# Router logits in four column groups, and the up product behind gate, in a fused decoder layer

## The reference

```python
x = layernorm(x + attn(x))                    # one head; theta from sigmoid, tanh, relu; softmax
x = layernorm(x + cross_attn(x, ctx))         # 16 heads of 16, within chunks of 64 tokens
x = layernorm(x + moe(x))

# moe, for each token:
logits = tokens @ router_weight.T             # 32 experts
scores = sigmoid(logits)
sfc    = scores + router_bias
# the best 2 of 4 groups of 8 experts, by the sum of their two best; in them the best 4 experts
topk_w = scores[topk] / scores[topk].sum() * 2.5
mixed  = sum_k topk_w[k] * down_k(silu(gate_k(t)) * up_k(t))
shared = (silu(t @ shared_gate_w.T) * (t @ shared_up_w.T)) @ shared_down_w.T
out    = mixed + shared
```

## Time and profile before

| | |
|---|---|
| time, median of 3 runs | 827.7 us (824.57 to 830.9) |
| profiled execution: span on the page | 830.3 us |
| PE busy | 765.2 us, 92% |
| VectorE busy | 581.5 us, 70% |
| ScalarE busy | 494.4 us, 60% |
| GpSimd busy | 368.0 us, 44% |
| mean granted TensorE clock | 0.969 |

### The profile page before, as it was taken

The page is one execution under the profiler, slowest core; times in us unless marked ns, Lnnn a source line. Parts: engine busy times, 40 slices in busy tenths (PEclk is TensorE's granted clock), DMA queues, the critical chain, the costliest instruction groups (busy, mean ns, idle before and its releaser), DMA issues.

```text
span 830.3 us, 21803 instructions
## 1 busy us (share of the span) xinstructions
PE 765.2 (92%) x8308; PEld 665.4 (80%) x8308; DVE 581.5 (70%) x2094; ACT 494.4 (60%) x1166; POOL 368.0 (44%) x437
## 2 busy tenths in 40 slices
PE   7969899999999999999997756799999999999986
PEld 6758788888888888888876636799999999998554
DVE  2345487898889888898888763366666666665486
ACT  0546666767767767777654414467676766764143
POOL 0101214334543355334554662366666666665142
PEclk9999999999999999999989877799999999999999
DMA  6582221332433334332113436755555555552996
GB/s 233 156 214 84 84 84 53 108 118 92 142 121 110 120 99 129 120 110 89 66 65 103 142 111 189 270 172 167 177 172 173 171 169 170 176 168 83 370 401 241
DMA packets 69642, 124.95 MB, mean 150 GB/s; under 512 B 9665, under 2 KB 43329, under 8 KB 69282
## 3 DMA queue, kind: packets, MB, share of 16 engines
q1 hardware_dynamic: 51394, 81.60, 32.1%
q0 software_dynamic: 13776, 37.77, 12.6%
q10 hardware_dynamic: 4368, 4.20, 1.4%
HBM read 73.16 MB, written 50.36 MB: 149 GB/s over the span
## 4 chain that ended last, share of the span: by engine, by line
PE 78%; DMA 7%; DVE 6%; SPq 5%; issue 2%; POOL 1%; ACT 1%; ACTq 0%; DVEq 0%
PE banks L538 17%; PE banks L284 10%; PE banks L545 8%; PE banks L386 3%; PE banks L377 3%; PE banks L354 3%; PE banks L322 3%; PE banks L367 3%; PE banks L489 3%; SPq L567 3%; PE banks L331 3%; PE banks L463 3%; PE banks L498 3%; PE banks L339 3%; DMA w_expert_tile<-y 2%; PE banks L429 2%
## 5 line engine op out<-in xcount | busy, mean ns | idle before, releaser
L1293 POOL DMA_INDIRECT y<-yb_tile,idcol_tile x159 | 152.4, 959 | 112.9 <-DVE yb_tile L1144 110.2
L538 PE MATMUL banks<-xbT_tile,wgu_tile 128*128 128x128 f32 x1272 | 172.0, 280 | 0.0
L538 PEld LDWEIGHTS banks<-xbT_tile,wgu_tile 128*128 128x128 f32 x1272 | 158.6, 196 | 0.1
L1144 DVE SCALAR_TENSOR_TENSOR yb_tile<-banks,rowsb_tile 128x256 f32<-128x256 f32 x159 | 76.9, 484 | 84.2 <-PE banks L545 76.1
L857 ACT ACTIVATE wgu_tile<-w_expert_tile 128x512 f32 x159 | 98.9, 622 | 11.8 <-DVE tab_i_tile L1121 11.8
L545 PE MATMUL banks<-w_expert_tile,hb_tile 128*128 x318 | 96.3, 385 | 5.2 <-DVE hb_tile L1132 5.2
L1271 POOL DMA_INDIRECT routed<-row_tile,idx_tile x64 | 62.5, 976 | 68.8 <-PE banks L399 53.2
L853 ACT ACTIVATE gb_tile<-banks 128x128 f32<-128x128 f32 x159 | 44.1, 277 | 79.1 <-PE banks L538 79.1
L1265 POOL DMA_INDIRECT routed<-row_tile,idx_tile x64 | 61.7, 964 | 31.1 <-issue 18.5
L1246 POOL TENSOR_TENSOR rs_tile<-ve_tile,half_neg_tile 128x2 f32<-128x2 f32 x16 | 11.1, 693 | 143.6 <-DVE ve_tile L960 143.6
L284 PE MATMUL banks<-const_tile,rowsb_tile 128*128 128x128 f32 x318 | 62.2, 278 | 7.1 <-DMA rowsb_tile<-routed 7.1
(11 more groups left out here) (206 smaller groups left out, 1784.4 us busy)
## 6 DMA issues: line engine op xcount, KB each, us to landing
rowsb_tile<-routed SPq DMA_DIRECT2D x159, 129.0 KB, 2.2
w_expert_tile<-y SPq DMA_DIRECT2D x15, 1024.0 KB, 15.0
w_expert_tile<-w_expert SPq DMA_DIRECT2D x16, 768.0 KB, 4.6
cT_tile<-ctxT SPq DMA_DIRECT2D x16, 384.0 KB, 3.2
routed<-zrow_tile SPq DMA_DIRECT2D x1, 4128.0 KB, 22.5
xT_tile<-xT SPq DMA_DIRECT2D x16, 256.0 KB, 3.0
x_sb_tile<-x SPq DMA_DIRECT2D x16, 256.0 KB, 2.7
inner<-hs_tile SPq DMA_DIRECT2D x16, 256.0 KB, 2.3
```

The source lines that it names most:

```text
L538: m = e.matmul(bank[2 + u % 4][:, h * P:(h + 1) * P], wgu[u % WG][:, k * D + h * EI:k * D + (h + 1) * EI], xbT[u % 2][:, k * P:(k + 1) * P ...
L1144: e.scalar_tensor_tensor(yb[n % YS][:, :], bank[6 + u % 2][:, 0:D], rowsb[n % ROWS][:, D:D + 1], rowsb[n % ROWS][:, 0:D], ALU.mult, ALU.ad ...
L1293: e.indirect_dma_start(y, bass.IndirectOffsetOnAxis(ap=idcol[n % ROWS][:, :], axis=0), yb[n % YS][:, :], None).then_inc(SEM[f"st_y{n % YS} ...
```

## The change

Four things, in the routing of one sequence:

1. `pe_router`: before, four products with 128 token columns of x2 as the loaded weights and the 32 router columns as the moving operand; the output has tokens on partitions, 64 columns. Now eight products with the 32 router columns as loaded weights and 64 tokens moving, into four groups of 32 partitions; the output has experts on partitions.
2. `act_sc` takes the tanh of that output into `lg`, which shares its memory with `g8` of the routing, so it now waits for the routing of the sequence before (`v_route`). Then PE brings it back to token rows by two products with pieces of the identity (`pe_scT`), placed behind the scores of the first attention, and DVE makes the sigmoid out of PSUM in a stage of its own (`vec_sc`), placed behind `vec_shb`. Before, that instruction stood at the head of `vec_route`.
3. `pe_up` waits for `v_sc` in place of `a_sc`.
4. `pe_up` moves from in front of `pe_pTa` to behind `pe_gate`.

```diff
         def pe_router(e, i):
             e.wait_ge(SEM["a_x2T"], i + 1)
             e.wait_ge(SEM["ld_w"], 16 * 3)
-            for t in range(T):
-                for k in range(DK):
-                    m = e.matmul(bank[7][:, t * E:(t + 1) * E], x2T[i % 2][:, k, t * P:(t + 1) * P], w_router[:, k, :],
+            for k in range(DK):
+                for j in range(4):
+                    m = e.matmul(bank[7][32 * j:32 * j + 32, 0:CH], w_router[:, k, :], x2T[i % 2][:, k, j * CH:(j + 1) * CH],
                                  start=k == 0, stop=k == DK - 1)
             m.then_inc(SEM["p_router"], 1)
+
+        def pe_scT(e, i):
+            e.wait_ge(SEM["a_sc"], i + 1)
+            own = ident.rearrange("p (t a x) -> p a t x", t=T, a=2)
+            for a in range(2):
+                m = e.matmul(bank[7][a * CH:(a + 1) * CH, CH:CH + T * E], lg[:, :], own[:, a, :, :], start=True, stop=True)
+            m.then_inc(SEM["p_scT"], 1)
...
         def pe_up(e, i):
-            after(e, SEM["a_sc"], min(i + 2, nseq))
+            after(e, SEM["v_sc"], min(i + 2, nseq))
             after(e, SEM["v_hs"], i)
...
-                if live(t - 5):
-                    pe_up(e, t - 5)
+                if live(t - 4):
+                    pe_scT(e, t - 4)
                 if live(t - 2):
                     pe_pTa(e, t - 2)
                 if live(t - 4):
                     pe_gate(e, t - 4)
+                if live(t - 5):
+                    pe_up(e, t - 5)
...
         def act_sc(e, i):
             e.wait_ge(SEM["p_router"], i + 1)
-            e.activation(sc[:, :, :].rearrange("p a b -> p (a b)"), bank[7][:, 0:T * E], ACT.Tanh, scale=0.5)\
+            after(e, SEM["v_route"], i)
+            e.activation(lg[:, :], bank[7][:, 0:CH], ACT.Tanh, scale=0.5)\
                 .then_inc(SEM["a_sc"], 1)
...
+        def vec_sc(e, i, ch):
+            e.wait_ge(SEM["p_scT"], i + 1)
+            e.tensor_scalar(sc[:, :, :].rearrange("p t x -> p (t x)"), bank[7][:, CH:CH + T * E], 0.5, 0.5,
+                            ALU.mult, ALU.add).then_inc(SEM["v_sc"], 1)
+
         def vec_route(e, i, ch):
 
-            e.wait_ge(SEM["a_sc"], i + 1)
-            ch(e.tensor_scalar(sc[:, :, :], sc[:, :, :], 0.5, 0.5, ALU.mult, ALU.add))
+            e.wait_ge(SEM["v_sc"], i + 1)
...
                 if live(t - 2):
                     vec_shb(e, t - 2, ch)
+                if live(t - 4):
+                    vec_sc(e, t - 4, ch)
                 if live(t):
                     vec_th(e, t, ch)
```

More of the change, by code:

```diff
@@ L35 @@
     "p_av1", "p_av2", "p_den", "p_down", "p_gu", "p_k", "p_out2", "p_pTa", "p_pTb", "p_prT", "p_q", "p_rank",
-    "p_router", "p_s1", "p_s2", "p_setup", "p_sg", "p_spread", "p_su", "p_sum", "p_tab", "p_vo", "p_x1T", "p_x2T",
+    "p_router", "p_s1", "p_scT", "p_s2", "p_setup", "p_sg", "p_spread", "p_su", "p_sum", "p_tab", "p_vo", "p_x1T", "p_x2T",
     "p_xbT", "p_z", "st_hs", "st_zrow", "v_adr", "v_fve", "v_h1", "v_hb", "v_hb1", "v_hs", "v_key", "v_msel",
-    "v_mx", "v_mxa", "v_mxb", "v_nblk", "v_nmr", "v_o", "v_onehot", "v_own", "v_r", "v_rden", "v_rep", "v_route",
+    "v_mx", "v_mxa", "v_mxb", "v_nblk", "v_nmr", "v_o", "v_onehot", "v_own", "v_r", "v_rden", "v_rep", "v_route", "v_sc",
     "v_setup", "v_sha", "v_shb", "v_sum", "v_tab", "v_ve1", "v_ve2", "v_yb", "v_zrow",
@@ L202, in build @@
         g8 = sa("g8", [P, T, GRP, 8])
+        lg = g8[:, :, :, :].rearrange("p t g x -> p (t g x)")
         gs = sa("gs", [P, T, GRP + 6])
```

## The result

The changed kernel took 839.7 us (median of four runs, 835.9 to 840.8), the kernel before 828.1 beside it (824.6 to 830.9). The ratio is **1.013, with an interval of 1.009 to 1.017**: slower by about 1.3%.

The account below looks back on a forecast made before the run. PE was taken to bound the kernel, with up filling its wait for DVE's shb. Terms -0.25 + 1.5 + 4.7 + 2.6 + 2.5 - 1.7 = +9.3 us, against 827.7, gave 837.0 us; range 829 to 842.

Parts of the forecast that it names:

- iteration 4: First step, no up yet: DVE had waited 0.53 us for PE's vo, which the shorter router brings forward; -0.25 us.
- iteration 5: Step where the transposes have only 0.37 us behind shb: the wait saves 0.22, up adds 1.73; +1.5 us.
- iteration 16: Late step where PE already waited 0.92 us for shb: up adds 1.73 to 3.46 us, 2.6 taken.
- iteration 17: Late step where PE already waited 1.88 us for shb: up adds 1.4 us at full clock, 5.5 at slow; 2.5 taken.
- iteration 19: Late step on a slow clock: gate comes without up in front, so gated values are earlier; -1.7 us.
- up behind the wait: Iterations 6 to 15: up no longer covers PE's wait for DVE's shb; 26.85 us against 26.38, +0.47 each, +4.7 in all.
- The router and the way back: PE's own work: router 0.81 to 0.56 us, identity products 0.45 to 0.77; net +0.35, costed at nothing in full iterations.
- PE's order alone sets the pace: Rival: shb's wait does not bind and tiling has no borders; -0.46 us in each of 16 iterations, 820.3 us; chance 0.06.
- third rival: Sixteen router passes at full-pass cost put PE 1.2 us beyond the wait at the transposes; 853 us, chance 0.07.
- up is covered after all: Rival: transposes bound later than shb, or slack behind them takes up 0.47 us; 832 us, no change; chance 0.22.
- the column groups don't overlap: Rival on the new router: sixteen passes at 0.10 us make it 1.6 us; +1.6 us in each of 16 iterations; chance 0.07.
- the change doesn't do what it says: Rival: up might still stand in front, or the sigmoid still behind, in PE's and DVE's instruction order; not counted.

## Why the prediction came out right

The forecast was 837.0 us and the time 839.7; the sum was +9.3 us on the profiled execution, and up to the key of iteration 19 it is 496.92 - 487.44 = +9.48. What follows that key takes 1.3 us less than before, with no edit in it (341.6 beside 342.9 us, where the second trace of the kernel before has 340.6), so that the spans differ by 8.2. That the sum is met to 0.2 us is partly luck, for two of its errors, +1.3 in iteration 16 and -1.7 in 19, cancel. Against the medians, which are 11.6 us apart, the forecast is 2.7 us short. In the table each key is compared with the same key of before.

| step | predicted | measured |
|---|---|---|
| iteration 4 | -0.25 | +0.56 |
| iteration 5 | +1.5 | +1.55 |
| iterations 6 to 15 | +4.7 | +4.24 |
| iteration 16 | +2.6 | +3.87 |
| iteration 17 | +2.5 | +2.77 |
| iteration 18 | 0 | -0.15 |
| iteration 19 | -1.7 | -3.36 |
| sum | +9.3 | +9.48 |

**The deciding term, up behind the wait, was right in mechanism and size.** Its four pieces came out as 9.70, 0.15, and 17.01 for the last two (predicted 9.71, 0.15, 15.26 + 1.73), 26.86 us in all. Three experiments stand behind it. The move alone gives the same 26.86. Another product in the place of up takes most of the iteration's loss away, 0.39 of 0.48 us with the old router. And DVE's work doubled ahead of shb lengthens the iteration by 1.26 us with the new order, by 0.02 with the old. The ten iterations have 4.24 rather than 4.7 us because neither trace is clean throughout: before has seven iterations of 26.41 to 27.04, after three of 27.37 to 27.71, and the excess is in the gaps of L455 and L456, 2.5 and 1.9 us in all. Clean against clean it is 0.48.

**Iteration 5** came out at +1.55, from the slack of 0.37 us that was read in the earlier trace rows. **Iteration 4** holds the start's scatter: it changed sign, but by less than the 1.0 us that the kernel before moves by itself. From the transposes of iteration 3, which leaves the start out, its key comes after 41.72 us, where it came after 42.10 and 42.24 in the two traces of before. So the predicted -0.25 is there, as -0.4 to -0.5.

**The router and the way back were mis-sized, in both halves.** From the start of the product z to that of the value-output product it takes 243.71 - 241.53 = 2.18 us, of which 1.73 is z's eight passes at full clock: the router with its two borders is 0.45 us, where 0.56 was predicted and 0.81 stood before. So 0.36 is saved, not 0.25. The two products with their borders are 193.59 - 191.50 = 2.09 us less 1.73, 0.36 us; the predicted range was 0.45 to 0.77. PE's own work so goes up by about nothing (0.03 by the pair of kernels with gate in front), where 0.35 was taken and 0.20 was the lower bound. What failed in the step is the price of a border. It was read as 0.19 us from the value product L354, and a 128x256 product in front of narrow work loses 0.09 here, 1.82 instead of 1.73; with the earlier trace rows alone the extra 0.19 could not be told from what L354 loses for other reasons. The error did not reach the sum, because the term was costed at nothing, as covered by the wait: the wait grew to 0.37 us instead of 0.1 to 0.3. The rival that PE's order alone sets the pace needed borders of under 0.1 us. The two borders of the router cost 0.45 - 0.23 = 0.22 us, and those of the products 0.36 - 0.12 = 0.24 if the four passes take the prediction's estimate of 0.12, so each costs some 0.11. That is near the rival's bound and far from its sum: PE's work did not go down by 0.46 us an iteration, it went up by 0.03. Its other condition failed outright, for shb was not earlier.

**The last iterations** were right in sum, by pieces that differ from those taken. From the transposes to the key, iteration 16 has up's 1.73 us more, and gate on the slow clock 441.82 - 438.46 = 3.36 us, 0.58 longer than before; the rest, 1.55 us, is in the narrow passes of L456, of which 21 come late. The chain shows it:

```profile
448.78 1.27 issue
```

Without that gap the step would be 2.60; the gap was no part of the prediction. It belongs to the new program and not to the order: from L456 to L387 iteration 16 takes 1.56 to 2.84 us in the four traces with the new router, and 1.00 to 1.04 in the ten with the old. (Iteration 6 is alike, 1.78 to 1.97 against 1.00 to 1.11.) Why the passes come late there stays open. That 2.60 is the number taken is luck, since the prediction had all of it in up, on a clock between half and full, and up took 1.73. In 17 the fall of the clock, which had been named as a bound worth 5.5, did come, but only part of it: from start to start the transposes take 1.73 us instead of 0.90, gate takes 466.58 - 464.07 = 2.51 instead of 1.90, while up has full clock again, 1.73. Less the 0.33 us of waiting for ACT that it fills, that is +2.84, and +2.77 was measured. In 19 the way from router to gate was taken to be 2.2 us and is 489.42 - 488.38 = 1.04, where it was 481.75 - 475.74 = 6.01: the router was taken to run on the slow clock, and here it ran at the full one. Its row has 0.43 us, as in iteration 9, and the granted clock was 0.95 from 485 to 490 us, where it was 0.50 from 475 to 480 before. Gate gives 1.5 us of that back, being 3.48 us instead of 1.94, near the 1.7 that the prediction took for it.

**Slips in the sums.** With 1.73 and 1.4 us for iterations 16 and 17 and 2.1 gained in 19, the lower bound adds to +7.0 and not +6.6. The upper price of iteration 17 is 1.4 + 4.33 = 5.7 and not 5.5. The third rival has PE 1.1 us behind shb and not 1.2. None of them moves the forecast or a chance.

**The chances.** The forecast of +1.1% was near the bound of 1%, and the chances for slower and for within 1% were 0.46 and 0.48. The measured +1.3% is beyond it, with an interval that reaches down to 0.9%. The forecast was nearer to the result than these chances were.

**The rivals.** That up is covered after all is refuted by the full iterations of 26.86 us, with a wait for shb in each; that the column groups don't overlap, by the 0.43 us of sixteen passes. That the change doesn't do what it says: both moves stand in the timeline.

Left open: how much of the loss is the last iterations' own. The tail is 68.9 us with up behind everywhere and 64.2 with up behind in full iterations only, 4.7 apart. But one order of the tail, that of the kernel before, gave 66.5, 66.0 and 64.2 in three traces, so some 2 us of it are not of the order's making.

## What to carry to other kernels

Before moving work on the bounding engine, look at what another engine finishes meanwhile: the distance between that end and the instruction that needs it (1.41 us here) is the slack, and if the work that covered it moves behind the wait, something about as long that does not wait must take its place, or the iteration can become as long as the ring through both engines. That sum, with four durations from two timelines, gave the iteration to 0.01 us, while the price of the edited operations themselves hardly mattered. Where a full pipeline and its last iterations are short of different things, their order can be chosen apart.

## What was not expected of the hardware

- **The borders to narrow work are cheap here.** In front of narrow work the same 128x256 product (z, or the scores) takes 1.82 us instead of 1.73. A tenth more is no sign of such a border by itself: gate takes 1.83 in front of the full-width transposes in the kernels with gate first. Sixteen passes of 32 columns with their way back to full width add 0.36 us, and four passes of 64 columns 0.26 to 0.27.
- **A small DVE instruction is long while POOL works.** L950 of the kernel before has 128x2 elements. It takes 0.16 us up to iteration 5 and 2.30 to 2.32 us in each of 6 to 15, where it ends within 0.04 us of POOL's additions. In the changed kernel the same instruction, L961, takes 0.20 to 0.22 us there. Whether POOL holds it was not tested. The rows are of the kernel before, iteration 10.

```profile
274.40 2.31 DVE L950 TENSOR_TENSOR nmx_tile<-mx_tile,tenth_neg_tile 128x2 f32<-128x2 f32 x1
...
275.27 1.40 POOL L1258 TENSOR_TENSOR xc_tile<-x_tile,c_out_tile 128x256 f32<-128x256 f32 x2
```

- **One chip was 4% slower for the same kernel** (863.0 beside 828 to 831 us). The iterations with "remote" waits are only a part of that: in the three kernels where only ACT had them, what follows the key of iteration 19 took 351 to 363 us, beside 340 to 344 for the same edits on the other chips, and the way to that key 3 to 13 us more. A comparison of less than 1% was not to be had there.
- **The start scatters by nearly 4 us** (the key of iteration 4 at 127.9 to 131.7) with the arrival of one early transfer (PE's wait 3.1 to 6.7 us), against some 9 that the whole change costs in the trace. Per-iteration distances are free of it; the time of a run isn't.
